# A graph network's dense attention stage: first product transposed with biases on partitions, no second turn, two steps of the norm on VectorE

## The reference

```python
out = node_attr @ cen_w + cen_b + aggr          # aggr: per head, sum over edges of alpha * (... @ wvl_w + wvl_b)
out = ssp(out) @ out_w + out_b                  # ssp(x) = softplus(x) - log 2
mu, var = mean(out), var(out)
y = (out - mu) / sqrt(var + 1e-05) * ln_g + ln_b
x = layernorm(x + y)                            # no weights
```

## Time and profile before

| | us |
|---|---|
| median of 3 runs | 9727.6 (9725.4 to 9736.0) |
| the profiled execution | 9720.8 |
| its span | 9719.1 |
| dense_attention in it | 6550 to 7645 |

### The profile page before, as it was taken

One profiled execution on the slowest core, in us unless ns is written; L12 is line 12 of the kernel. 1 busy time (PEld: TensorE's weight loads), 2 busy tenths in 40 slices (PEclk: granted clock), 3 DMA queues, 4 the chain that ended last, 5 costly groups with the idle time before them and its releaser, 6 DMA issues. The chain is left out here.

```text
span 9719.1 us, 128687 instructions
## 1 busy us (share of the span) xinstructions
PE 5035.1 (52%) x22317; PEld 4013.2 (41%) x22317; DVE 6701.7 (69%) x16290; ACT 3989.0 (41%) x10116; POOL 6541.4 (67%) x6395
## 2 busy tenths in 40 slices
PE   5220017677444664444477676766666566652222
PEld 1000015555333443222366666666666544442222
DVE  5776758888787665666688888879999644543333
ACT  0667846666222223444444444435555333321111
POOL 0776757777677666777666666655555677767777
PEclk7555558888555665555566666666666666655555
DMA  3000014444223443333211111112332344442222
GB/s 138 8 8 23 7 46 146 145 145 143 62 51 70 104 102 81 85 85 85 54 37 38 38 38 38 38 41 96 99 99 99 100 137 138 139 121 61 62 60 50
DMA packets 825286, 757.17 MB, mean 78 GB/s; under 512 B 451844, under 2 KB 567882, under 8 KB 821802
## 3 DMA queue, kind: packets, MB, share of 16 engines
q1 hardware_dynamic: 637068, 589.29, 19.7%
q0 software_dynamic: 188160, 167.28, 8.6%
HBM read 458.34 MB, written 309.38 MB: 79 GB/s over the span
## 5 line engine op out<-in xcount | busy, mean ns | idle before, releaser
L2653 DVE CUSTOM_DVE_ANT_0 att_junk<-bank,att_away 128x512 f32<-128x512 f32 x1568 | 977.9, 683 | 123.2 <-PE bank L2833 109.5
L996 PE MATMUL bank<-att_payload,att_match 128*128 128x68 f32 x3136 | 583.5, 365 | 196.3 <-issue 98.3
L996 PEld LDWEIGHTS bank<-att_payload,att_match 128*128 128x128 f32 x3136 | 571.7, 281 | 241.4 <-issue 241.4
L2592 POOL DMA_INDIRECT attn_tab<-att_new,att_put_i x392 | 386.5, 986 | 411.5 <-DVE att_new L2690 319.1
L472 POOL DMA_INDIRECT half_sorted<-ka_out_row,ka_put_i x392 | 397.2, 1013 | 281.6 <-ACT ka_put_i L605 167.3
L1045 POOL DMA_INDIRECT ga_ends<-x_tab,ga_src_i x392 | 417.4, 1065 | 213.4 <-ACT ga_src_i L1987 113.5
L675 POOL DMA_INDIRECT edges<-kb_out_row,kb_put_i x392 | 423.3, 1080 | 154.2 <-issue 122.2
L1045 POOL DMA_INDIRECT ma_ends<-in_x,ma_dst_i x392 | 418.9, 1069 | 119.5 <-issue 113.4
L1615 POOL DMA_INDIRECT x_tab<-mb_run,mb_put_i x392 | 400.3, 1021 | 142.9 <-issue 100.9
L3674 PE MATMUL bank<-ident,sb_pay 128*65 128x128 f32 x392 | 109.3, 433 | 746.4 <-DVE sb_pay L3561 746.4
L1045 POOL DMA_INDIRECT gb_ends<-h_tab,gb_src_i x392 | 391.8, 999 | 144.2 <-issue 118.5
(11 more groups left out here) (505 smaller groups left out, 19237.0 us busy)
## 6 DMA issues: line engine op xcount, KB each, us to landing
da_agg<-attn_tab SPq DMA_DIRECT2D x98, 288.0 KB, 2.9
attn_tab<-ka_attn_start SPq DMA_DIRECT2D x24, 1152.0 KB
x_tab<-ma_wide SPq DMA_DIRECT2D x98, 260.0 KB
ma_xn<-in_x SPq DMA_DIRECT2D x98, 256.0 KB
h_tab<-ma_h_out SPq DMA_DIRECT2D x98, 256.0 KB
attn_x<-ma_z_out SPq DMA_DIRECT2D x98, 256.0 KB
ga_same<-same_next SPq DMA_DIRECT2D x196, 128.0 KB, 2.9
gb_same<-same_prev SPq DMA_DIRECT2D x98, 256.0 KB
```

What stands on the lines that cost most here:

```text
L996: ins = self.nc.tensor.matmul(bank[:, u * w:(u + 1) * w], self.match[s][:, t, u * P:(u + 1) * P], self.payload[s][:, t, :], start=(t == 0) ...
L2592: nc.gpsimd.indirect_dma_start(st["attn_tab"], bass.IndirectOffsetOnAxis(ap=put_i[s][:, q:q + 1], axis=0), new[s][:, q, :], None, bounds_c ...
L2653: ins = nc.vector.tensor_tensor_reduce(junk[h % 2][:, q, :], logit_t[h % 2][:], away[s][:, q, :], 1.0, -2.0 * BIG, ALU.subtract, ALU.max, ...
```

## The change

The first product is formed transposed. x and the scaled values are turned as pairs of nodes (two groups of four transposes), copied, and multiplied with two block diagonal matrices as the weights, `w_centre` and `w_shares`, each over 512 columns, both into one bank. Features then lie on partitions, so `cen_b` is a per-partition operand of ScalarE's Abs and of VectorE's softplus step (`b_cen_off` is its negative, and what the maximum with it leaves is put right in `B_OUT`), and the softplus result is already turned for the second product: the second turn and its copy go. The bias `wvl_b` comes through x's last column, where VectorE writes the first head's share: x's columns sum to nothing, so `w_centre` holds `cen_w` less its last row, and `wvl_b` in that row. The weighing with `ln_g` moves from GpSimd to VectorE, beside the last scaling, which was there; GpSimd keeps `move_res` alone. `prepare_weights` loads 22 pieces for this where it loaded 10. The orders of all engines' steps are written anew; SyncE stores the result of n-1 first in its step, and loads x and the table for n+7.

The diff's core (the new step orders, and the operations that are added):

```diff
 # prepare_weights, SyncE
-            load(st["w_att_out"][0:D, :], a["L2_gnn_cen_w"])
-                load(BVL[o, o], a["L2_gnn_wvl_w"])
-                load(rows[:, R_["B_VL"], o], a["L2_gnn_wvl_b"].unsqueeze(0).broadcast_to([P, DH]))
+            for half in (0, D):
+                load(st["b_cen"][half:half + D, :], a["L2_gnn_cen_b"].unsqueeze(1))
+                load(CEN[half:half + D - 1, :], a["L2_gnn_cen_w"][0:D - 1])
+                load(CEN_LAST[half:half + D - 1, :], a["L2_gnn_cen_w"][D - 1:D].broadcast_to([D - 1, D]))
+                for h in range(H):
+                    o = slice(h * DH, (h + 1) * DH)
+                    load(CEN[half + D - 1:half + D, o], a["L2_gnn_wvl_b"].unsqueeze(0))
+                    b = slice(half + h * DH, half + (h + 1) * DH)
+                    load(st["w_shares"][b, b], a["L2_gnn_wvl_w"])
 # dense_attention, GpSimd
-                if there(n + 3, CHUNKS):
-                    make_bias(*ahead(n, i, s, 3))
-                if there(n + 4, CHUNKS):
-                    put_x(*ahead(n, i, s, 4))
                 if there(n + 1, CHUNKS):
                     move_res(*ahead(n, i, s, 1))
-                    weigh(*ahead(n, i, s, 1))
 # VectorE
-                nc.vector.tensor_tensor(part[s][:], hd[:, :, :, DH], recip[:], ALU.mult)
-                nc.vector.tensor_tensor(heads(both[s][:, :, D:P]), hd[:, :, :, 0:DH], per_head(recip[:]), ALU.mult
+                nc.vector.tensor_tensor(x[s][:, :, D - 1], hd[:, :, 0, DH], recip[:, :, 0], ALU.mult).then_inc(marked, 1)
+                nc.vector.tensor_tensor(heads(shares[s][:]), hd[:, :, :, 0:DH], per_head(recip[:]), ALU.mult
                                         ).then_inc(scaled, 1)
-                nc.vector.tensor_tensor(z[:], p1.result(s), bias[:], ALU.add).then_inc(added1, 1)
-                nc.vector.scalar_tensor_tensor(out=soft[:], in0=z[:], scalar=0.0, in1=e[:], op0=ALU.max, op1=ALU.add
+                nc.vector.scalar_tensor_tensor(out=soft[s][:], in0=join_b[s][:], scalar=st["b_cen_off"][:], in1=e[s][:],
+                                               op0=ALU.max, op1=ALU.add).then_inc(softened, 1)
+            def weigh(n, i, s):
+                dve.wait_ge(added2, n + 1)
+                if not fresh(n):
+                    dve.wait_ge(res_used, n - 1)
+                nc.vector.tensor_tensor(weighed[s][:], v[s][:], over_rows(rows[:, st["B_LNG"], :]), ALU.mult
+                                        ).then_inc(weighing, 1)
+            def step(n, i, s, first, last):
+                ln1.sum_squares(dve, n)
+                if not fresh(n, 1):
+                    finish(n - 1, i + s - 1, 1 - s)
+                if there(n + 5, CHUNKS):
+                    scale(*ahead(n, i, s, 5))
+                if there(n + 2, CHUNKS):
+                    soften(*ahead(n, i, s, 2))
+                norm1(n, i, s)
+                if there(n + 1, CHUNKS):
+                    add2(*ahead(n, i, s, 1))
+                    weigh(*ahead(n, i, s, 1))
+                ln2.sum_squares(dve, n)
 # ScalarE
+            def copy(n, s):
+                act.wait_ge(x_turned, n + 1)
+                if not fresh(n):
+                    act.wait_ge(joined, n - 1)
+                nc.scalar.activation(x_t[s][:], x_b[s][:], ACT.Copy)
+                act.wait_ge(shares_turned, n + 1)
+                nc.scalar.activation(shares_t[s][:], shares_b[s][:], ACT.Copy).then_inc(copied, 1)
+            def step(n, i, s, first, last):
+                if not fresh(n, 1):
+                    ln2.take_root(act, n - 1)
+                ln1.take_root(act, n)
+                if there(n + 3, CHUNKS):
+                    log_part(n + 3, 1 - s)
+                ln2.squares(act, n, y[s][:])
+                if there(n + 1, CHUNKS):
+                    ln1.squares(act, n + 1, v[1 - s][:], added2)
+                if there(n + 5, CHUNKS):
+                    copy(n + 5, 1 - s)
 # TensorE
+            def join(n, s):
+                pe.wait_ge(copied, n + 1)
+                if not fresh(n):
+                    pe.wait_ge(softened, n - 1)
+                nc.tensor.matmul(join_b[s][:], st["w_centre"][:], x_t[s][:], start=True, stop=False)
+                nc.tensor.matmul(join_b[s][:], st["w_shares"][:], shares_t[s][:], start=False, stop=True
+                                 ).then_inc(joined, 1)
+            def step(n, i, s, first, last):
+                if there(n + 1, CHUNKS):
+                    multiply(n + 1, 1 - s)
+                if there(n + 5, CHUNKS):
+                    turn(n + 5, 1 - s)
+                if there(n + 4, CHUNKS):
+                    join(n + 4, s)
```

More of the change, by code:

```diff
@@ L332, in _ @@
             take(rows[:, R_["B_OUT"], :], b[:, 0:D])
+            take(rows[:, R_["B_OUT"], :], b[:, 0:D], add=rows[:, R_["B_OUT"], :])
             take(st["b_mix1"][0:D, :], b[0:D, 0:1])
@@ L2487, in product_program @@
-def product_program(pe, st, pr, rows, ready, weight, read):
-    def turn(n, i, s):
-        for sem, value in ready(n, i, s)[:-1]:
-            pe.wait_ge(sem, value)
-        pr.turn(pe, n, s, rows[s], ready(n, i, s)[-1])
-    def step(n, i, s, first, last):
-        if there(n + 1, st["CHUNKS"]):
-            turn(*ahead(n, i, s, 1))
-        pr.multiply(pe, n, s, weight, read)
-    turn(0, 0, 0)
-    over_pairs(pe, st["CHUNKS"], step)
 def flat(ap):
@@ L2857, in dense_attention @@
 def dense_attention(nc, st):
-    CHUNKS, bank, rows = st["CHUNKS"], st["bank"], st["rows"]
+    CHUNKS, bank, rows, ident = st["CHUNKS"], st["bank"], st["rows"], st["ident"]
     HW = DH + 1
@@ L2901, in load_res, with store @@
                 sp.dma_start(flat(res[s][:]), table_rows(st["attn_x"], first_node(st, n))).then_inc(res_in[s], 16)
-            def step(n, i, s, first, last):
-                if there(n + 6, CHUNKS):
-                    load(n + 6, s)
-                if there(n + 2, CHUNKS):
-                    sp.wait_ge(res_used, n + 1)
-                    load_res(n + 2, s)
+            def store(n, i, s):
                 sp.wait_ge(finished, n + 1)
@@ L3082, in step @@
-            def step(n, i, s, first, last):
-                ln1.squares(act, n, v[s][:], added2)
-                if there(n + 2, CHUNKS):
-                    log_part(n + 2)
+            def copy(n, s):
+                act.wait_ge(x_turned, n + 1)
+                if not fresh(n):
+                    act.wait_ge(joined, n - 1)
+                nc.scalar.activation(x_t[s][:], x_b[s][:], ACT.Copy)
+                act.wait_ge(shares_turned, n + 1)
+                nc.scalar.activation(shares_t[s][:], shares_b[s][:], ACT.Copy).then_inc(copied, 1)
@@ L3103, in _ @@
+            copy(3, 1)
+            ln1.squares(act, 0, v[0][:], added2)
+            copy(4, 0)
+            over_pairs(act, CHUNKS, step, tail=6)
+            ln2.take_root(act, CHUNKS - 1)
         @block.tensor
         def _(pe):
-            def turn1(n, s):
-                pe.wait_ge(scaled, n + 1)
-                p1.turn(pe, n, s, both[s], (x_put, n + 1))
-            def multiply1(n, s):
-                p1.multiply(pe, n, s, st["w_att_out"][:], added1)
-            def turn2(n, s):
-                p2.turn(pe, n, s, soft, (softened, n + 1))
@@ new lines, in join, with multiply @@
+            def join(n, s):
+                pe.wait_ge(copied, n + 1)
+                if not fresh(n):
+                    pe.wait_ge(softened, n - 1)
+                nc.tensor.matmul(join_b[s][:], st["w_centre"][:], x_t[s][:], start=True, stop=False)
+                nc.tensor.matmul(join_b[s][:], st["w_shares"][:], shares_t[s][:], start=False, stop=True
+                                 ).then_inc(joined, 1)
+            def multiply(n, s):
+                pe.wait_ge(softened, n + 1)
+                if not fresh(n):
+                    pe.wait_ge(added2, n - 1)
+                for r in range(4):
+                    ins = nc.tensor.matmul(out_b[s][:, r * P:(r + 1) * P], soft[s][:, r * P:(r + 1) * P], st["w_out"][:],
+                                           start=True, stop=True)
+                ins.then_inc(mapped, 1)
@@ L3133, in _ @@
-            turn1(2, 0)
-            multiply2(0, 0)
-            turn2(1, 1)
-            multiply1(2, 0)
-            over_pairs(pe, CHUNKS, step)
+                    multiply(n + 1, 1 - s)
[3 more added lines that the diff above has]
+                    join(n + 4, s)
+            for n in (0, 1, 2):
+                turn(n, n % 2)
+                if n < 2:
+                    join(n, n)
+            turn(3, 1)
@@ L3140, in sage_first @@
+            join(2, 0)
+            multiply(0, 0)
+            turn(4, 0)
+            join(3, 1)
+            over_pairs(pe, CHUNKS, step, tail=6)
 def sage_first(nc, st, dest):
```

227 lines of the change are left out of this document (65 added, 162 removed).

## The result

| | before | after |
|---|---|---|
| median of 4 runs, us | 9728.3 (9725.4 to 9736.0) | 9500.5 (9498.9 to 9512.9) |
| the profiled execution, its span | 9720.8, 9719.1 | 9501.5, 9499.4 |
| ratio of the times | | 0.9767 (95%: 0.9751 to 0.9784) |
| dense_attention, first instruction to the next stage's first | 1097.7 | 856.1 |
| one chunk of it | 10.87 | 8.44 |

The kernel is faster by 2.3%.

The account below looks back on a forecast made before the run. VectorE, standing partly behind GpSimd, was taken to bound the kernel. 97 chunks going from 10.87 to 8.44 us (-236) plus 7 of preparation gave -229: a median of 9498.6 us, range 9445 to 9582.

Parts of the forecast that it names:

- The mechanism: In dense_attention VectorE sets the pace and stands still behind GpSimd inside its own instructions, 2.5 us of a 10.87 us chunk.
- the prediction's four parts: VectorE's standing behind GpSimd per chunk: 1.06 us in softplus step, 0.72 in share, 0.45 in scaling, 0.27 in reciprocal's first.
- the signs of being right: Scaling every 8.4 us; no 128x512 VectorE instruction above 0.75; 0.4 idle before last scaling; one GpSimd instruction of 1.27.
- VectorE's own work: Sum of VectorE's instructions in one new chunk by start-to-start distances, without the wait for ScalarE: 8.02 us.
- The wait for the root: VectorE waits ahead of the last scaling for ScalarE's root, 0.42 us a chunk, bounds 0 and 0.6.
- the copies' price: ScalarE's two PSUM copies ahead of the root, 0.59 us each, ending at about 4.05 us after the residual addition.
- Cost nothing, with 0.3 us of margin: GpSimd's residual addition runs from about 2.8 to 4.2 us, beside the sums of squares, and delays no VectorE instruction.
- rival (a): Residual lands 0.8 us later, GpSimd's addition meets the last scaling: 0.85 us a chunk, +82 us, 9581; chance 15%.
- TensorE: 8.0 us forecast: TensorE's chunk: 1.9 us of transposes, 1.9 of second product, 4.2 of first product; still under VectorE's 8.4.
- The join: TensorE's transposed first product, four new 512-column instructions at 1.06 us each, 4.2 us a chunk, within 2.4 to 4.9.
- Rival (d): TensorE becomes the bound: 11.6 us a chunk, 9803 us, chance 3%; milder at 9 to 10, 9550 to 9650, 5%.
- Preparation: +7 us forecast: Before VectorE's first work, 12 more small loads at 0.42 or 0.60 us plus three small operations: +7 us.

Follow-up runs that it names:

- quiet: The kernel before without three of GpSimd's instructions per chunk (two bias steps, the addition to the residual); 9474.3 us against 9704.9, ratio 0.9765.
- company: The kernel after with three GpSimd instructions per chunk added, on tiles that nobody else uses; 9602.6 us against 9704.9 before, ratio 0.9892.
- residual_early: soften_first with GpSimd's residual addition released by the weighing, from a residual loaded one step sooner, into its own tile; 9457.7 us against 9722.4 before, 0.9726.
- soften_first: The kernel after with VectorE's softplus step moved ahead of the last scaling; 9459.8 us, ratio 0.9743 to the kernel before.

## Why the prediction was right, point by point

**The mechanism was right.** VectorE set the pace, and stood behind GpSimd inside its own instructions; `quiet` and `company` show it from both sides. 2.5 us were put on it; `quiet` gave back 2.27 with 0.25 of new meetings in its last scaling, 2.5 together, and its four rows give the prediction's four parts: 1.06, 0.72, 0.45 and 0.27. Of the signs of being right, the 8.44 us and GpSimd's one instruction of 1.27 us came; the idle time was 0.25 us instead of 0.4, and that no VectorE instruction of 128x512 would last over 0.75 us was wrong, by the last scaling.

**VectorE's own work: 8.02 us forecast, 8.01 measured** (`residual_early`, with the same instructions in another order). Within it the softplus step is 0.66 us to the next start (7012.21 to 7012.87) instead of 0.61: with a PSUM source and a pointer it lasts 745 ns, the upper bound, where I took the lower. The share's product is 0.09 (7011.52 to 7011.61) instead of 0.13.

**The wait for the root: 0.42 us forecast, 0.32 measured.** The two sums of squares leave VectorE free to start at 7008.54 + 1.20 = 7009.74; it starts at 7010.06. Counted from the end of the residual addition (7005.64), VectorE is ready at 4.10, forecast 4.08. The root ends at 4.32 and the scaling starts at 4.42, where 4.5 was forecast with the handovers: the two copies start 0.47 us apart (7008.47, 7008.94, 7009.42), where each was priced at 0.59 and hardly any overlap. So the two copies end at 3.89 instead of 4.05. The step that was off is the copies' price, put too close to their duration.

**"Cost nothing, with 0.3 us of margin" was wrong, in the form of rival (a), mildly.** The residual's load takes 3.0 us instead of 2.6, with 127 GB/s flowing instead of 99. The traffic alone isn't the reason, for in `residual_early` it takes 2.6 us at 134 GB/s; there it is issued some 5 us behind the loads of x and the table, here 0.8 us behind the latter (7005.82, 7004.99), and no run separates the two. GpSimd runs from 3.55 to 4.81 on that clock (7009.19 to 7010.45, less 7005.64), where 2.8 to 4.2 was forecast; it starts 0.87 us ahead of the last scaling here and 1.35 ahead (7000.23, 7001.58) one chunk earlier. The last scaling is 789 ns on average instead of 691: 0.10 us a chunk, not (a)'s 0.85. The rival took it that all chunks meet alike; these two differ by 0.48 us, and over the window the start is 0.2 to 0.9 us later than the 2.8 forecast, so that at most the last 0.56 us of GpSimd's instruction are met. The sum closes within 0.01: 8.01 + 0.32 + 0.10 = 8.43 of 8.44.

**TensorE: 8.0 us forecast, 5.8 measured** (408.66 us in 600, 71 chunks), which cost nothing as it was covered in either case. The join's four instructions last 1039 and 906 ns and overlap, (131.2 + 112.9) / 70 = 3.5 us a chunk against 4.2; the eight records of the second product are 300 ns and come to 1.2 us, where 1.9 was priced; the transposes come to 1.8 for 1.9. These groups overlap each other for some 0.7 us more. The join's price was from a later stage, whose granted clock is lower (7700 to 8600 us before: 0.66, here 0.75). Rival (d) did not come.

**Preparation: +7 us forecast, +2.2 measured.** The loads that were added take 0.26 and 0.32 us and a gap of some 0.04, not 0.42 and 0.60. I priced twelve small loads by the rows of two that they replace; 34.31 to 34.97 us shows the pair at 0.66. By the timelines, the last load's issue starts 3.4 us later (31.61 before, 34.97 after), but VectorE follows it after 1.5 us instead of 2.7, and this second part was in no term.

**What was in no term.** dense_attention's first instruction is 15.8 us later than before: 1.5 at the start of `spread_mean`, 17.9 in it, 3.6 less between it and dense_attention. The stages behind dense_attention take 6.1 more, unexplained as the 3.6. In the stage the chunks gave 97 x 2.43 = 236, as forecast, and its fill 6 more: the first norm's scaling comes 28.4 us after the stage's start (6565.9 to 6594.3) instead of 34.2. So -241.6 in the stage and +21.9 outside make the -219.7 of the profiled span, where -236 + 7 = -229 was forecast; the medians differ by 227.7. The prediction's last digits are luck: -6 of fill, -5 of preparation and +20 elsewhere stood against each other, and the medians lie closer to it than the profiled execution.

## What to carry to other kernels

When a VectorE instruction is longer than others of its form and shows no idle time in front, look at what GpSimd does at its end: if it ends about its own length after GpSimd's, the time is GpSimd's, and GpSimd's instructions count on VectorE's path though it isn't the busy engine. Then either take them off, or put them beside VectorE work that reads PSUM or reductions with one input, but not beside a tensor_scalar in SBUF, which stood still with one input (0.45 us instead of 0.17). Here VectorE's new order was worth 0.22 us a chunk on top of the change (8.44 to 8.22, `soften_first`), and the place for GpSimd's addition 0.21 more (8.22 to 8.01, `residual_early`). Judge the halves of such a change together: one of them was a loss alone.

## What was not expected of the hardware

The pace of GpSimd's indirect transfers in one stage (972 or 983 to 985 ns an issue at the median, 18 us of 525) changes with what GpSimd's program has in a later stage: with three instructions of 0.19 us, whose results nobody reads, in each step of a later loop, the whole program was 21 us faster. And the granted clock of TensorE in the stage (a mean over time at 1.2 and at 2.4 GHz, as a share of the latter) was 0.62 before, 0.75 after and 0.84 in `residual_early`. The shorter weight loads don't explain it: in `quiet`, with the old products and with matmuls and weight loads busy for 70% and 67% of the window (68% and 66% before), it was 0.76. It isn't the pace alone either: `company`, at 9.91 us a chunk, has 0.75 as the kernel after. What raises it is open.
